# A ring of three bias tiles, copied for each tile of tokens, in place of all eight experts' biases held in SBUF

## The reference

```
x = x + tanh(g_xattn) * retention(layernorm(x), ctx, ctx)       # x: 8 x 256 x 256
xf = layernorm(x).reshape(2048, 256)
scores = softmax(xf @ Wg.T); w, idx = top_k(scores, 2); w = w / sum(w)
for each expert e of 8 (all have W1, W3: 512x256, W2: 256x512, each with a low-rank part of rank 16):
    h1 = xf @ W1[e].T + (xf @ A1[e].T) @ B1[e].T + b1[e]         # b1, b3: 512 numbers
    h3 = xf @ W3[e].T + (xf @ A3[e].T) @ B3[e].T + b3[e]
    g  = silu(h1) * h3
    y[e] = g @ W2[e].T + (g @ A2[e].T) @ B2[e].T + b2[e]         # b2: 256 numbers
x = x + tanh(g_ffn) * sum over the token's two experts of w * y[e]
```

## Time and profile before

| | |
|---|---|
| median of 3 runs | 345.79 us (345.37 to 346.42) |
| the profiled execution | 345.23 us, of which the span from first to last instruction is 343.4 us |
| mean granted TensorE clock | 0.968 of full speed |
| busy, share of the span | PE 90%, DVE 76%, POOL 57%, ACT 53% |
| DMA queues | q1 (started by SP) 28.52 MB, q0 (started by POOL) 9.36 MB, q10 (ACT) 5.52 MB |
| batches, 0 to about 119 us | attention and merging of weights |
| routing, about 119 to 141 us | the biases are copied meanwhile |
| tiles, about 141 us to the end | 39 tiles |

### The profile page before, as it was taken

One profiled execution on the slowest core, in us unless ns is written; L12 is line 12 of the kernel. 1 busy time (PEld: TensorE's weight loads), 2 busy tenths in 40 slices (PEclk: granted clock), 3 DMA queues, 4 the chain that ended last, 5 costly groups with the idle time before them and its releaser, 6 DMA issues.

```text
span 343.4 us, 6837 instructions
## 1 busy us (share of the span) xinstructions
PE 308.8 (90%) x1766; PEld 234.3 (68%) x1766; DVE 259.2 (76%) x638; ACT 183.2 (53%) x387; POOL 194.2 (57%) x171
## 2 busy tenths in 40 slices
PE   8589989999997377999999999999999999999970
PEld 3468777778886324467777777777777777777750
DVE  2679797879996599278877788778877788777850
ACT  4646655666775611265565555655565555655540
POOL 1459886878988616514564556554564556454331
PEclk9899999899999769999999999999999999999997
DMA  7937799899878269403332233333331333234100
GB/s 239 383 79 228 233 295 267 243 269 281 267 224 268 92 154 390 137 12 63 49 51 53 48 63 45 52 61 59 60 46 37 63 60 46 50 57 60 19 0 0
DMA packets 28098, 43.82 MB, mean 128 GB/s; under 512 B 6960, under 2 KB 15536, under 8 KB 27792
## 3 DMA queue, kind: packets, MB, share of 16 engines
q1 hardware_dynamic: 15888, 28.52, 26.5%
q0 software_dynamic: 7488, 9.36, 17.0%
q10 hardware_dynamic: 4688, 5.52, 5.1%
HBM read 31.43 MB, written 10.65 MB: 123 GB/s over the span
## 4 chain that ended last, share of the span: by engine, by line
PE 63%; POOL 9%; DVE 8%; DMA 8%; issue 4%; ACT 4%; SPq 1%; POOLq 1%; ACTq 0%; DVEq 0%
PE bank L497 31%; PE bank L514 15%; POOL WL L700 5%; DMA xs<-x_in 5%; PE bank L505 5%; PE bank L487 2%; PE bank L345 2%; DMA WH<-lora_in 2%; DVE stage L783 2%; ACT WH L578 2%; PE bank L443 1%; PE bank L388 1%; PE bank L450 1%; DVE st L798 1%; PE bank L404 1%
## 5 line engine op out<-in xcount | busy, mean ns | idle before, releaser
L761 POOL DMA_INDIRECT out<-ys,sidx x39 | 61.9, 1586 | 85.6 <-DVE gsel L1010 61.8
L700 POOL TENSOR_TENSOR WL<-stage,WH 128x512 bf16<-128x512 f32 x48 | 60.4, 1279 | 18.1 <-ACT WH L578 17.8
L497 PE MATMUL bank<-WH,xh 128*128 x156 | 56.0, 440 | 0.6 <-ACT xh L658 0.6
L685 ACT ACTIVATE ys<-BB,gsel 128x256 f32 x39 | 19.8, 509 | 55.0 <-DMA out<-ys,sidx 52.9
L497 PE MATMUL bank<-WH,xl 128*128 x156 | 48.9, 394 | 0.0
L751 POOL DMA_INDIRECT xg<-xn_rows,gidx x39 | 38.8, 995 | 15.2 <-issue 12.4
L497 PE MATMUL bank<-WL,xb 128*128 x156 | 47.3, 385 | 0.0
L578 ACT ACTIVATE WH<-stage 128x512 fp32r<-128x512 f32 x48 | 29.6, 631 | 22.4 <-DVE stage L783 22.2
L1025 DVE TENSOR_TENSOR h<-bank,BB 128x512 f32<-128x512 f32 x39 | 27.0, 691 | 15.7 <-PE bank L497 15.6
L664 ACT ACTIVATE gh<-bank 128x512 fp32r<-128x512 f32 x39 | 23.4, 599 | 26.8 <-PE bank L505 26.8
L497 PEld LDWEIGHTS bank<-WH,xl 128*128 128x128 f32 x156 | 29.2, 188 | 7.7 <-DVE xl L1016 0.5
(11 more groups left out here) (132 smaller groups left out, 598.0 us busy)
## 6 DMA issues: line engine op xcount, KB each, us to landing
stage<-w_all_in SPq DMA_DIRECT2D x48, 256.0 KB, 4.1
BB<-biases_in SPq DMA_DIRECT2D x8, 640.0 KB, 9.1
LS<-WH SPq DMA_DIRECT2D x45, 48.0 KB
xs<-x_in SPq DMA_DIRECT2D x8, 256.0 KB, 4.0
cx<-ctxT_in SPq DMA_DIRECT2D x8, 256.0 KB, 4.5
out<-x ACTq DMA_DIRECT2D x8, 256.0 KB, 3.9
xn_rows<-xn ACTq DMA_DIRECT2D x8, 256.0 KB, 5.1
lora_parts<-WH ACTq DMA_DIRECT2D x3, 432.0 KB, 5.2
```

Of the source, the lines that this page charges most:

```text
L497: last = nc.tensor.matmul(dst[:, :], lhs[p][:, c * P:(c + 1) * P], W[:, bass.ds(e * (UNITS * UC) + (2 * kind + c) * UC, HID)], start=(part ...
L700: nc.gpsimd.tensor_tensor(w_dst(WL, s, m), stage[(u * UNITS + m) % NSTAGE][:], w_dst(WH, s, m).bitcast(F32), ALU.subtract).then_inc(s_wl, 1)
L761: nc.gpsimd.indirect_dma_start(out=out_rows, out_offset=bass.IndirectOffsetOnAxis(ap=sidx[:, i:i + 1], axis=0), in_=ys[p][:], in_offset=No ...
```

## The change

SP no longer loads the biases ahead of the tiles. It waits for `s_routed`, and then for each tile i reads the expert's number into a register, and copies that expert's 1280 biases into buffer i % 3 of a ring (`BB[0..2]`, one semaphore each). From the fourth tile on it first waits until tile i - 3 has used its b3 (`s_h3b`) and its b2 (`s_b2g`). The gate weights are now written before any bias is loaded. ACT and DVE no longer read the expert's number; each waits in each tile for the ring's buffer. So 39 copies of 640 KB take the place of 8.

```diff
-        BB = sb(whole, "BB", [P, E, BCOL])
+        BB = [sb(whole, f"BB{r}", [P, BCOL]) for r in range(BRING)]
...
-            for e in range(E):
-                sp.dma_start(BB[:, e, :], biases[e:e + 1, :].to_broadcast([P, BCOL])).then_inc(s_bb, 16)
-                if e == 0:
-                    sp.wait_ge(s_gates, 1)
-                    sp.dma_start(xn2_d[:, D:D + K].rearrange("(j p) k -> p j k", p=P), gate[:]).then_inc(s_gates_d, 16)
+            sp.wait_ge(s_gates, 1)
+            sp.dma_start(xn2_d[:, D:D + K].rearrange("(j p) k -> p j k", p=P), gate[:]).then_inc(s_gates_d, 16)
+
+            def load_biases(i):
+
+                r = i % BRING
+                if i == 0:
+                    sp.wait_ge(s_routed, 1)
+                if i >= BRING:
+                    sp.wait_ge(s_h3b, i - BRING + 1)
+                    sp.wait_ge(s_b2g, i - BRING + 1)
+                e = sp.value_load(eid[0:1, i:i + 1], min_val=0, max_val=E - 1)
+                sp.dma_start(BB[r][:], biases[bass.ds(e, 1), :].to_broadcast([P, BCOL])).then_inc(s_bb[r], 16)
+
+            for i in range(NT_SLOTS):
+                load_biases(i)
...
-                e = act.value_load(eid[0:1, i:i + 1], min_val=0, max_val=E - 1)
                 act.wait_ge(s_gs, i + 1)
+                act.wait_ge(s_bb[i % BRING], 16 * (i // BRING + 1))
                 if i >= 2:
                     act.wait_ge(s_scat[p], 16 * half(i, p))
-                nc.scalar.activation(ys[p][:], BB[:, bass.ds(e, 1), 2 * HID:BCOL].rearrange("p o d -> p (o d)"), ACT.Copy,
+                nc.scalar.activation(ys[p][:], BB[i % BRING][:, 2 * HID:BCOL], ACT.Copy,
                                      scale=gs[q]).then_inc(s_b2g, 1)
...
-                e = dve.value_load(eid[0:1, i:i + 1], min_val=0, max_val=E - 1)
...
+                dve.wait_ge(s_bb[i % BRING], 16 * (i // BRING + 1))
+                biased(h1, pH1, i, 0, s_h1, s_h1b)
...
-            dve.wait_ge(s_bb, 16 * E)
```

More of the change, by code:

```diff
@@ L45 @@
 KJ = K * NJ
+BRING = 3
 EPS = 1e-5
@@ L192, in flamingo @@
         s_r = sem("s_r")
-        s_bb = sem("s_bb")
+        s_bb = [sem(f"s_bb{r}") for r in range(BRING)]
         s_h1b, s_h3b, s_b2g = sem("s_h1b"), sem("s_h3b"), sem("s_b2g")
@@ L679, in tile @@
                 nc.scalar.activation(h1[:], h1[:], ACT.Silu).then_inc(s_silu, 1)
-                e = act.value_load(eid[0:1, i:i + 1], min_val=0, max_val=E - 1)
                 act.wait_ge(s_gs, i + 1)
+                act.wait_ge(s_bb[i % BRING], 16 * (i // BRING + 1))
                 if i >= 2:
                     act.wait_ge(s_scat[p], 16 * half(i, p))
-                nc.scalar.activation(ys[p][:], BB[:, bass.ds(e, 1), 2 * HID:BCOL].rearrange("p o d -> p (o d)"), ACT.Copy,
+                nc.scalar.activation(ys[p][:], BB[i % BRING][:, 2 * HID:BCOL], ACT.Copy,
                                      scale=gs[q]).then_inc(s_b2g, 1)
             act.wait_ge(s_routed, 1)
-            act.wait_ge(s_bb, 16 * E)
             x_parts(0, 0)
@@ L1020, in g_rest, with biased, product @@
                 nc.vector.tensor_tensor(gl[:], pG[:, :], gh[:].bitcast(F32), ALU.subtract).then_inc(s_gl, 1)
-            def biased(dst, src, i, e, kind, ready, sig):
+            def biased(dst, src, i, kind, ready, sig):
                 dve.wait_ge(ready, i + 1)
[L1024 to L1028, removed]
+                nc.vector.tensor_tensor(dst[:], src[:, :], BB[i % BRING][:, kind * HID:(kind + 1) * HID], ALU.add).then_inc(sig, 1)
+            def product(i):
+                biased(g, pH3, i, 1, s_h3, s_h3b)
                 dve.wait_ge(s_silu, i + 1)
@@ L1044, in tile @@
                 pos_wait(dve, s_g, i)
-                biased(h1, pH1, i, e, 0, s_h1, s_h1b)
+                dve.wait_ge(s_bb[i % BRING], 16 * (i // BRING + 1))
+                biased(h1, pH1, i, 0, s_h1, s_h1b)
                 if not first:
@@ L1049, in tile @@
                     x_rest(i + 1, 1 - p)
-                product(i, e)
+                product(i)
                 if not first:
```

## The result

The changed kernel takes 394.33 us (median of 4 executions, 392.7 to 397.0) against 346.11 us (4 executions of the kernel before): 1.140 times as long, with a 95% interval of 1.134 to 1.147. The forecast of 370 us had the sign, the chain that is hit, and half the size; 394 lies outside its range.

A forecast was written before the change was run, and what follows sets the result against it. PE bounds the kernel at 4.83 us a tile, scatters close behind at 4.68. Tiles 25.5 + 1.8 - 1.5 - 1.3 = 24.5 us, plus 0.6 at the start, on 345.23 gave 370 us, range 347 to 385.

The forecast's parts named there:

- What bounds the kernel: In the tiles: PE at 4.83 us a tile, with a second chain of scatters able to run at 4.68.
- When the copy's data begin: In a tile: copy issued 1.3 us after the landing of the awaited scatter, data moving from about 2.3 to 4.0.
- Does it add up: Whether copy and scatter, sharing the DMA engines, take the sum of their times; assumed yes, delaying the scatter 1.0 us.
- The first rival: In the tiles: the copy hardly delays the scatter, at most 0.21 us by short queue turns; 346 to 349 us, 19 in 100.
- The length of the copy: One 640 KB copy fills all 16 DMA engines for 1.70 us at 386 GB/s.
- d: How much later a full tile's scatter lands because of the copy; taken as 1.0 us, bounds nothing to 1.7.
- The nearly empty tiles: Two tiles with short scatters, said to meet the copy for 0.2 us and give back 0.75 us each, 1.5 us.
- The three smaller ones: Three tiles with scatters 0.15 us shorter, said to cost 0.6 us each, 1.8 us.
- The store of 1.3 us: In the tiles: lateness of a scatter absorbed before PE stops, 0.7 plus 0.6 us; subtracted once from the sum.
- The start: First tile: three copies run beside the first gathers and delay them 0.6 us, bounds nothing to 1.7.
- What is removed: Register loads and checks on ACT and DVE, and copies under the routing: counted nothing, 0.2 us at most in the last tile.
- The range: Forecast span for the whole kernel, 347 to 385 us, leaving out 15 in 100 below and 5 above.

The follow-up runs named there:

- e5_32: Changed kernel, but from the fourth tile each copy moves only 32 columns (16 KB); 352.35 us against 346.48 for the kernel before, ratio 1.019.
- e2_late: Changed kernel, each copy from the fourth on also waiting for Silu of tile i - 2; 352.45 us against 345.20 for the kernel before, ratio 1.018.
- e6_start: e2_late with the first copy issued earlier, second and third after the first tile's transposes; 351.63 us against 346.48 for the kernel before, ratio 1.011.
- e9_far32: e6_start with copies of 32 columns (16 KB) from the fourth tile on; 346.85 us against 345.66 for the kernel before, ratio 1.002.
- e4_spread: Changed kernel with biases laid out 128 times in DRAM, each partition filled from its own row; 393.73 us against 345.20 for the kernel before.
- e7_mid: Changed kernel, each copy from the fourth on held until ACT has rounded g (s_gh); median 389.11 us against 346.48 for the kernel before.

## Why the prediction was wrong

**What bounds the kernel: right.** PE's 4.83 us a tile and behind it the scatters' chain at 4.68, with 0.15 us to spare. Everything that followed hangs on it: in `e5_32`, 16 KB a tile lengthen the chain by 4.1 us.

**When the copy's data begin: right.** Forecast L + 2.3, L being the landing. In the tile above L is about 228.7 (ACT starts `ys` at 228.80), the copy is issued at 230.11 and its traffic begins in the slice from 231.0: L + 2.3. SP's register load, priced by ACT's, was priced well.

**Does it add up: right in direction, and as a queue.** I left open whether the scatter waits or shares. The trace shows the copy first, nearly whole, and then the scatter. Of the rule of the Trainium skill, "DMA: Bandwidth & Descriptors", section "Queues, rings and completion order", that an engine takes turns between queues by packets, the tile shows no turn for the scatter in the stretch from 231.7, when its data would have begun, to 233.2. The first rival, which rested on short turns, is out by 45 us. It had counted the scatter's 8 rows on an engine as one turn but the copy's turn as one row. With the 9 to 17 descriptors to a turn that the Trainium skill gives there, and a row taken as a descriptor, the copy's 8 rows on an engine are less than one turn as well, and the trace agrees with that reading; no run here tests it.

**The length of the copy: wrong, and this is the step that failed.** "At the 386 GB/s that such copies moved alone it fills all 16 DMA engines for 1.70 us." That is the rate of seven copies in a row. In the tile a single copy took 2.7 us, its packets being slow at first. The kernel before had a better number: its first bias copy, alone on the queue, moved from 121.15 to about 123.3 us. Two stretches of it, 121.15 to 122.5 us and 122.5 to 123.2 us:

```profile
DMA packets 82, 0.42 MB, mean 311 GB/s; under 512 B 0, under 2 KB 0, under 8 KB 82
```

```profile
DMA packets 47, 0.20 MB, mean 285 GB/s; under 512 B 8, under 2 KB 8, under 8 KB 47
```

That is nearly the whole copy in 2.05 us, so some 2.2 us in all. (Its landing, 4.0 us after its issue, would mislead: the gate weights' small packets stood behind it in the same queue from 123.3 us on.) With 2.2 us in place of 1.7, the prediction's own sum gives d = 1.5 us in place of 1.0. In the tile shown the copy had 2.1 us left when the scatter was due, and the scatter's first data were late by 1.5, since the last 18 rows let it run beside them. The full tiles say the same: a link of the chain takes 6.17 us, 1.5 more than 4.68. So d was 1.5 us, and the full tiles cost 39.3 us in place of 25.5. These 13.8 us are most of the 19.6 us by which the tiles and the end together took more than forecast (44.1 against 24.5).

**The nearly empty tiles: wrong, by the same step.** I let them give back 1.5 us. They cost 1.7, 3.2 us more. I had the copy meet them for 0.2 us, but a scatter of about ten rows waits for the copy as one of 128 does: the one at 204.72 landed in 4.9 us, where the same tile's took 3.0 us in `e2_late`, and is followed 5.70 us later. The three smaller ones cost 3.5 us in place of 1.8.

**The store of 1.3 us: there, and worth little.** In a tile of the middle, `down` starts 1.56 us after the scatter before the change (230.38 and 231.94) and 0.55 after it (229.51 and 230.06): 1.0 us of the store is used. But the kernel before had used most of it too by the end, where its scatters ran late by themselves: at the thirty-sixth `down` starts 0.76 us after the scatter before the change (322.96 and 323.72) and 0.54 after it (370.83 and 371.37). So the end came 0.4 us earlier in place of 1.3.

**The start: mis-sized.** 2.0 us in place of 0.6, and 0.3 beyond the upper of the bounds that I gave (nothing to 1.7 us). `e6_start` shows that it comes from the copies ahead of the first gather, as I took it to.

**What is removed: right.** Nothing, by `e9_far32`'s chain of scatters.

**The range.** Its upper end of 385 us rested on a chance of 5 in 100 for a d of 1.7. With the length of the copy too short by 0.5 to 1.0 us, a d of 1.5 was the likely case and not the tail. And the 1.5 us by which routing ended later add to the miss in the profiled execution; they were no part of any term.

What is left open: why a single copy of 640 KB takes 2.2 to 2.7 us where a steady stream takes 1.7. `e4_spread` excludes the shared source row. And why even a small copy costs a scatter 0.2 us.

## What to carry to other kernels

Ask of added DMA traffic not how much it is but what is in flight at that moment, and look for serial chains of DMAs (a scatter that waits for the scatter before) that run just under the pace of the engine that seems to bound the kernel: their spare time is in no table of busy shares. Price a transfer that stands alone by one that stood alone, from its first data to its last, not by the rate of a stream.
If such traffic must run in a tile, tie its start to a signal that comes after the critical DMA's data both when the kernel is on time and when it is late; one extra wait was worth 41 of 48 us here.

## What the runs showed of the hardware

A DMA that the one queue had begun held back another queue's for much of its length: a median of 1.4 us for 640 KB, and still 0.2 us for 16 KB. A single 640 KB copy moved at 256 GB/s while it kept the engines 96% busy, a stream of such copies at 386 GB/s at 98%. Two orders of the same transfers, 4.83 and about 6.8 us a tile, were each stable for many tiles of one execution (`e7_mid`), so that a kernel can look settled at either. And the batches ahead of the tiles, the same code in all kernels, ended at times up to 4 us apart in single executions, which can hide effects of 1 to 2 us from a median of four; distances within the tiles of one trace leave this part out.
